# Context projection of the first pair first, eight early maxima of the second unit, one transpose for a unit's maxima

## The reference

```python
x = _layernorm(builder_state, g1, beta1)
base_n = _layernorm(base_state, g1, beta1)
q, k, v = (heads(q_in, Wq, bq), heads(kv_in, Wk, bk), heads(kv_in, Wv, bv))
scores = jnp.einsum('bhqd,bhkd->bhqk', q, k) * (1.0 / np.sqrt(HD))
attn = jax.nn.softmax(scores, axis=-1)
out = jnp.einsum('bhqk,bhkd->bhqd', attn, v)
x = residual + (out @ W_o.T + b_o)
U = (_layernorm(x, g2, beta2) @ W_in.T + b_in) @ Bmat
s = jax.nn.silu(s @ A.T) + u_t          # a scan over the rows
return x + states @ Cmat + mod
```

## Time and profile before

| what | value |
|---|---|
| median of three runs | 2315.91 us (2312.77 to 2317.89) |
| the profiled execution | 2315.49 us, span of its instructions 2313.7 us |
| TensorE busy | 2254.5 us, 97% of the span |
| VectorE busy | 1733.4 us, 75% |
| GpSimd busy | 1583.7 us, 68% |
| ScalarE busy | 1110.4 us, 48% |
| mean granted TensorE clock | 0.989 |

### The profile page before, as it was taken

The page is one execution under the profiler, slowest core; times in us unless marked ns, Lnnn a source line. Parts: engine busy times, 40 slices in busy tenths (PEclk is TensorE's granted clock), DMA queues, the critical chain, the costliest instruction groups (busy, mean ns, idle before and its releaser), DMA issues.

```text
span 2313.7 us, 36253 instructions
## 1 busy us (share of the span) xinstructions
PE 2254.5 (97%) x14262; PEld 1306.4 (56%) x14262; DVE 1733.4 (75%) x2167; ACT 1110.4 (48%) x1422; POOL 1583.7 (68%) x1039
## 2 busy tenths in 40 slices
PE   8999989999999999999999999999999999999987
PEld 8998854554555544555555455555555555445764
DVE  5765446888888778888888788888888888755865
ACT  3654424445445445444454544544544545453454
POOL 1200026888888888888888888888888888887312
PEclk8999999999999999999999999999999999999998
DMA  6660225677777777777777777677677776787723
GB/s 241 211 193 10 83 64 118 147 160 159 157 160 155 165 167 171 174 158 161 157 159 169 174 174 173 156 166 158 151 158 162 161 160 155 185 186 172 240 100 145
DMA packets 159703, 365.02 MB, mean 158 GB/s; under 512 B 23535, under 2 KB 63087, under 8 KB 158894
## 3 DMA queue, kind: packets, MB, share of 16 engines
q0 software_dynamic: 59904, 218.13, 46.2%
q1 hardware_dynamic: 99630, 144.59, 19.3%
HBM read 95.41 MB, written 49.02 MB: 62 GB/s over the span
## 4 chain that ended last, share of the span: by engine, by line
PE 81%; DMA 5%; POOL 4%; issue 4%; DVE 4%; ACT 1%; POOLq 0%; SPq 0%; DVEq 0%; ACTq 0%
PE ps L1303 28%; PE ps L1176 10%; PE ps L1278 7%; PE ps L1280 7%; PE ps L1282 7%; DMA acca<-pt 5%; PE ps L1140 4%; PE ps L1270 4%; PE ps L1158 3%; PE ps L1148 3%; POOL accp L533 3%; PE ps L1368 2%; PE ps L1121 1%; DVE mx_part L922 1%; PE ps L1425 1%
## 5 line engine op out<-in xcount | busy, mean ns | idle before, releaser
L715 ACT ACTIVATE pt<-ps 128x1024 f32<-128x1024 f32 x800 | 779.3, 1021 | 908.5 <-PE ps L1282 878.2
L922 DVE TENSOR_REDUCE mx_part<-ps 128x2 f32<-128x1024 f32 x768 | 938.0, 1221 | 338.5 <-PE ps L1176 338.4
L533 POOL TENSOR_TENSOR accp<-accp,pt 128x1024 f32<-128x1024 f32 x416 | 1040.5, 2501 | 220.7 <-ACT pt L715 219.0
L1303 PE MATMUL ps<-pt,v 128*64 128x512 f32 x3328 | 805.6, 605 | 0.0
L995 DVE TENSOR_TENSOR ps<-ps,shb 128x1024 f32<-128x1024 f32 x403 | 493.1, 1224 | 52.1 <-PE ps L1282 52.1
L1303 PEld LDWEIGHTS ps<-pt,v 128*64 128x64 f32 x3328 | 201.8, 136 | 344.0 <-issue 335.3
L1176 PE MATMUL ps<-kk,qh 64*128 64x512 f32 x1536 | 349.0, 450 | 10.0 <-DVE mx_part L922 10.0
L1176 PEld LDWEIGHTS ps<-kk,qh 64*128 64x128 f32 x1536 | 143.3, 183 | 355.2 <-DVE mx_part L922 268.6
L1278 PE MATMUL ps<-qh,kk 64*128 64x512 f32 x1664 | 328.8, 391 | 6.9 <-ACT pt L715 6.9
L1280 PE MATMUL ps<-qh,kk 64*128 64x512 f32 x1664 | 328.5, 390 | 0.0
L1282 PE MATMUL ps<-ql,kk 64*128 64x512 f32 x1664 | 328.2, 389 | 0.0
(11 more groups left out here) (154 smaller groups left out, 1898.3 us busy)
## 6 DMA issues: line engine op xcount, KB each, us to landing
acca<-pt POOLq DMA_DIRECT2D x224, 512.0 KB, 4.9
accb<-pt POOLq DMA_DIRECT2D x160, 512.0 KB, 4.8
q_scratch<-kk SPq DMA_DIRECT2D x32, 512.0 KB, 4.4
acca<-accp POOLq DMA_DIRECT2D x32, 512.0 KB, 4.6
o_scratch<-ost SPq DMA_DIRECT2D x32, 512.0 KB, 3.0
og<-o_scratch SPq DMA_DIRECT2D x32, 512.0 KB, 5.9
shb<-m_scratch SPq DMA_DIRECT2D x31, 512.0 KB, 4.1
xs<-x SPq DMA_DIRECT2D x16, 512.0 KB, 6.4
```

Of the source, the lines that this page charges most:

```text
L533: nc.gpsimd.tensor_tensor(acc[:, :], acc[:, :], pt[n % PT_SLOTS][:, :], ALU.add).then_inc(added_p, 1)
L715: nc.scalar.activation(pt[n % PT_SLOTS][:, :], src, ACT.Exp, scale=SCALE).then_inc(exped, 1)
L922: nc.vector.tensor_reduce(mx_part[:, m % QT, :, m // QT], src, AX_X, ALU.max).then_inc(max_taken, 1)
L1303: ins = mm(ps[HD * h:HD * (h + 1), 6, :], v[:, t, f:f + HD], pt[n % PT_SLOTS][:, h * QB:(h + 1) * QB], start=(t == 0), stop=(t == NT - 1))
```

## The change

- The chunks of K are projected in the order of the pairs, 2, 3, 0, 1. ScalarE's wait for the stored q in group 0 moves ahead of its first V copy.
- Eight maxima of unit 1 join those of unit 0 in the projection (`ctx_maxima`, 34 in all, `M_EARLY`): two in group 2, three in groups 3 to 11, five in the last. In a group the first stands behind the second K chunk, the second behind the second V product, the third behind the fourth K chunk. VectorE takes the first ahead of its four `low_k`, and the second and third behind them. All early maxima use banks 5 and 6. The eight have q in a tile of their own, `qx`, loaded behind `qh` of unit 0. `mx_part` gets a second buffer.
- In the last group the K chunks come first, with maxima between them, then V for the first half, the turn of unit 0's maxima, and V for the second half. ScalarE does `shift(0)` before both copies of V.
- Every unit, unit 0 too, has two maxima in each step: 18 of unit 1 and eight of unit 2 in unit 0. In its first step both tiles' scores stand ahead of the shift matmuls. The turn is at step 9 in every unit.
- `mx_row` is [128, 2 x 4], and a single transpose gives eight rows of 128 (bank 7, for unit 0 bank 0). ScalarE negates these into `shift_row`; SyncE stores them to DRAM, waits, and loads the two rows of 512 into `sh` (`send_shift`), and loads `shb` as before (`spread_shift`).

```diff
 M_LEAD = 4
-M_FIRST = NM + 2 * M_LEAD
+M_EARLY = NM + 2 * M_LEAD
 
 
 def maxima_of(u, j):
 
-    if u == 0:
-        first, last = M_FIRST * j // NJ, M_FIRST * (j + 1) // NJ
-    else:
-        first = M_FIRST + 2 * (NJ * (u - 1) + j)
-        last = first + 2
-    return [(i // NM + 1, i % NM) for i in range(first, min(last, NM * (UNITS - 1)))]
-
-
-def turn_step(u):
-
-    return NJ - M_LEAD if u else NM * NJ // M_FIRST + 1
+    first = M_EARLY + 2 * (NJ * u + j)
+    return [(i // NM, i % NM) for i in range(first, min(first + 2, NM * UNITS))]
+
+
+TURN_STEP = NJ - M_LEAD
...
+def ctx_maxima(g):
+
+    if g < 2:
+        return []
+    if g == C_G - 1:
+        return [(0, m) for m in range(21, NM)]
+    third = [(1, g - 3)] if 3 <= g < C_G - 2 else [(0, 20)] if g == C_G - 2 else []
+    return [(0, 2 * (g - 2)), (0, 2 * (g - 2) + 1)] + third
+
+
+EARLY = [p for g in range(C_G) for p in ctx_maxima(g)]
+
+
+def nth_max(w, m):
+
+    return EARLY.index((w, m)) if (w, m) in EARLY else NM * w + m
...
+def max_bank(w, m):
+
+    return 5 if (w, m) in EARLY else 4
+
+
+def turn_bank(w):
+
+    return 7 if w else 0
...
-        mxp = at("mxp", [P, QT, HD + 1], RR + 11776)
-        mx_part = at("mx_part", [P, QT, 2, 7], RR + 12040)
+        mx_row = at("mx_row", [P, 2, QT], RR + 11776)
+        mx_part = [at("mx_part0", [P, QT, 2, 7], RR + 12032), at("mx_part1", [P, QT, 2, 7], RR + 11784)]
+        shift_row = at("shift_row", [2 * QT, P], RR + 11840, F32R)
+        qx = at("qx", [P, QB], RR + 12096, F32R)
         oraw = at("oraw", [P, QB], RR + 12096)
-        lnb = at("lnb", [P, 64], RR + 12096)
+        lnb = at("lnb", [P, 64], RR + 11968)
...
             def store_k(g):
                 for p in (0, 1):
-                    sp.wait_ge(k_ready, FC * g + (p + 1))
+                    sp.wait_ge(k_ready, FC * g + PAIR_ORDER.index(p) + 1)
                     keys = slice(g * GW, (g + 1) * GW)
                     sp.dma_start(k_scratch[p][:, :, keys], kk[:, p, :, keys].bitcast(F32)).then_inc(k_stored, 16)
 
+            def send_shift(w):
+                sp.wait_ge(shift_ready, w + 1)
+                wait(sp, sh_loaded, 16 * (w - 1))
+                wait(sp, shb_loaded, 16 * (w - 2))
+                sp.dma_start(m_scratch[w % 2].rearrange("h (q k) -> (h q) k", k=P), shift_row[:, :].bitcast(F32)).then_inc(sh_stored, 16)
+                sp.wait_ge(sh_stored, 16 * (w + 1))
+                sp.dma_start(sh[w % 2][0:HD + 1:HD, :].bitcast(F32), m_scratch[w % 2]).then_inc(sh_loaded, 16)
+
             def spread_shift(w):
-                sp.wait_ge(shift_ready, w + 1)
-                sp.dma_start(m_scratch[w % 2], sh[w % 2][0:HD + 1:HD, :].bitcast(F32)).then_inc(sh_stored, 16)
-                sp.wait_ge(sh_stored, 16 * w)
                 wait(sp, shifted, tiles_added(w - 1))
...
+                    b, p = unit(1)
+                    sp.dma_start(qx[:, :].bitcast(F32), q_scratch[b, 0, p]).then_inc(qx_loaded, 16)
...
-            sp.wait_ge(proj_done, projected(NG - 1))
+            sp.wait_ge(proj_done, projected(NG - 1) - 2)
             load_ql(0)
             for w in (1, 2):
                 load_qh(w)
             store_k(C_G - 1)
+            sp.wait_ge(ones_set, 3)
+            send_shift(0)
...
+                    send_shift(u + 1)
                     spread_shift(u + 1)
...
             def take_v(g, t):
-                act.wait_ge(proj_done, projected(X_G + g - 1) + (1, 4)[t])
+                act.wait_ge(proj_done, projected(X_G + g - 1) + ((1, 4)[t] if g < C_G - 1 else (5, 6)[t]))
                 nc.scalar.activation(v[:, GT * g + t], ps[:, 7, :], ACT.Copy).then_inc(v_ready, 1)
 
-            def high_k(g, c):
-                act.wait_ge(proj_done, projected(X_G + g - 1) + (2, 3, 5, 6)[c])
-                nc.scalar.activation(kk[:, c, 0, g * GW:(g + 1) * GW], ps[:, 2 + c % 3, 0:GW], ACT.Identity,
+            def high_k(g, i):
+                c = PAIR_ORDER[i]
+                act.wait_ge(proj_done, projected(X_G + g - 1) + ((2, 3, 5, 6)[i] if g < C_G - 1 else i + 1))
+                nc.scalar.activation(kk[:, c, 0, g * GW:(g + 1) * GW], ps[:, 2 + i % 3, 0:GW], ACT.Identity,
                                      bias=bqkv[:, 1, c:c + 1]).then_inc(k_hi, 1)
+
+            def shift(w):
+                act.wait_ge(max_turned, w + 1)
+                wait(act, sh_stored, 16 * w)
+                nc.scalar.activation(shift_row[:, :], ps[0:2 * QT, turn_bank(w), 0:P], ACT.Copy, scale=-1.0)\
+                    .then_inc(shift_ready, 1)
 
             act.wait_ge(cols_loaded, 16)
             act.wait_ge(w_loaded[0], 16)
                     if g == 0:
                         act.wait_ge(bias_ready, 2)
                         act.wait_ge(wkv_lo, 2 * FC)
-                    take_v(g, 0)
-                    high_k(g, 0)
-                    if g == 0:
                         for half in (0, 1):
                             act.wait_ge(q_stored[half], 32 * (X_G // 2))
-                    high_k(g, 1)
-                    take_v(g, 1)
-                    high_k(g, 2)
-                    high_k(g, 3)
-
-
-            def shift(w):
-                act.wait_ge(max_turned, w + 1)
-                if w == 0:
-                    act.wait_ge(ones_set, 3)
-                nc.scalar.activation(sh[w % 2][0:HD + 1, :], ps[0:HD + 1, 7, :], ACT.Copy, scale=-1.0)\
-                    .then_inc(shift_ready, 1)
+                    if g < C_G - 1:
+                        take_v(g, 0)
+                        high_k(g, 0)
+                        high_k(g, 1)
+                        take_v(g, 1)
+                        high_k(g, 2)
+                        high_k(g, 3)
+            for i in range(FC):
+                high_k(C_G - 1, i)
+            shift(0)
+            for t in range(GT):
+                take_v(C_G - 1, t)
...
-            def low_k(g):
-                for c in range(FC):
-                    dve.wait_ge(k_hi, FC * g + (c + 1))
-                    nc.vector.scalar_tensor_tensor(out=kk[:, c, 1, g * GW:(g + 1) * GW], in0=ps[:, 2 + c % 3, 0:GW],
-                                                   scalar=bqkv[:, 1, c:c + 1],
-                                                   in1=kk[:, c, 0, g * GW:(g + 1) * GW].bitcast(F32),
-                                                   op0=ALU.add, op1=ALU.subtract).then_inc(k_ready, 1)
-
-            def take_max(w, m, i):
+            def low_k(g, i):
+                c = PAIR_ORDER[i]
+                dve.wait_ge(k_hi, FC * g + (i + 1))
+                nc.vector.scalar_tensor_tensor(out=kk[:, c, 1, g * GW:(g + 1) * GW], in0=ps[:, 2 + i % 3, 0:GW],
+                                               scalar=bqkv[:, 1, c:c + 1],
+                                               in1=kk[:, c, 0, g * GW:(g + 1) * GW].bitcast(F32),
+                                               op0=ALU.add, op1=ALU.subtract).then_inc(k_ready, 1)
+
+            def take_max(w, m):
                 if m == 0:
-                    wait(dve, max_ready, w)
-                dve.wait_ge(max_done, NM * w + (i + 1))
-                src = ps[:, 5:7, :] if w == 0 else ps[:, 4:6, :]
+                    wait(dve, max_ready, w - 1)
+                dve.wait_ge(max_done, nth_max(w, m) + 1)
+                b = max_bank(w, m)
...
             def row_max(w):
-                dve.wait_ge(max_taken, NM * (w + 1))
+                dve.wait_ge(max_taken, NM * (w + 1) if w else M_EARLY)
                 wait(dve, max_turned, w)
-                nc.vector.tensor_reduce(mxp[:, :, 0:HD + 1:HD], mx_part[:, :, :, :], AX_X, ALU.max).then_inc(max_ready, 1)
+                nc.vector.tensor_reduce(mx_row[:, :, :].rearrange("p h q -> p q h"), mx_part[w % 2][:, :, :, :], AX_X, ALU.max)\
+                    .then_inc(max_ready, 1)
...
-                    if g >= 2:
-                        take_max(0, 2 * (g - 2), 2 * (g - 2))
-                    low_k(g)
-                    if g >= 2:
-                        take_max(0, 2 * (g - 2) + 1, 2 * (g - 2) + 1)
-            for m in range(2 * (C_G - 2), NM):
-                take_max(0, m, m)
+                    early = ctx_maxima(g)
+                    if g < C_G - 1:
+                        for w, m in early[:1]:
+                            take_max(w, m)
+                        for i in range(FC):
+                            low_k(g, i)
+                        for w, m in early[1:]:
+                            take_max(w, m)
+            for i in range(FC):
+                take_max(*ctx_maxima(C_G - 1)[i])
+                low_k(C_G - 1, i)
+            take_max(*ctx_maxima(C_G - 1)[FC])
             row_max(0)
...
-            def maxima(w, m, i):
-
-
-                wait(pe, max_taken, NM * w + i)
-                if i == 0:
+            def maxima(w, m):
+
+                wait(pe, max_taken, nth_max(w, m))
+                if m == 0 and w == 1:
+                    pe.wait_ge(qx_loaded, 16)
+                elif m == 0 or (w, m) == (1, 2 * M_LEAD):
```

(97 more changed lines are left out.)

30 lines of the change are left out of this document (14 added, 16 removed).

## The result

The changed kernel takes 2320.43 us, the median of 20 runs (2316.32 to 2325.8), against 2315.78 us for the kernel before in as many runs on the same chip: ratio 1.0024 (1.0016 to 1.0032). It is a quarter of a per cent slower. The forecast was 0.17% faster, so the sign is wrong, by 8.4 us.

The account below looks back on a forecast made before the run. TensorE was taken to bound the projection and units 1 to 31, with waits only in the tail and unit 0. From 2315.5 us, -12.4 + 24.3 + 0.3 - 11.4 - 5.7 + 1.4 = -3.5 gave 2312 us, range 2303 to 2324.

Parts of the forecast that it names:

- A: Unit 0, steps 1 to 12: two maxima per step in place of mostly three, 52.8 us against 65.2, -12.4 us.
- B: Context groups 3 to 11: a third maximum costs 0.42 us plus a 2.28 us wait for VectorE, +24.3 us.
- E: End of group 11: one clock fall of 3.4 us, +1.4 us; the other groups keep the full clock.
- Rival 1: Context groups: the clock falls in every group's stall, eight falls more, +13.6 us, 2325.7 us; chance 0.15.
- C: Turns in units 1 to 30: one transpose in place of four saves 0.38 us each, -11.4 us.
- Rival 2: The turn: a lone transpose hides in the switch, -20.4 us in place of -11.4, put at 2305 us; chance 0.18.
- D: Tail, last group's start to step 1 of unit 0: 22.7 us in place of 28.4, -5.7 us.
- Rival 4: Shift row through DRAM: late in every unit behind POOL's accumulations, 0.5 us in 31 units, 2327 us; chance 0.05.
- Rival 3: Context groups: no stall, because VectorE gets to the second maximum sooner, 2290 us; chance 0.09.

Follow-up runs that it names:

- the four useless matmuls: The changed kernel with four matmuls whose result nothing uses ahead of the third early maximum in groups 3 to 11: 2316.59 us, ratio 1.0004 to the kernel before.
- the turn alone: The kernel before with only one transpose in place of four and the shift row through DRAM, in every unit: 2304.03 us, ratio 0.9949.
- the orders without the stall: Changed kernel, VectorE taking the second maximum before the third chunk's low part: 2293.7 us; also with TensorE's second maximum between third and fourth K products: 2292.33 us.

## Why the prediction was wrong

**A, unit 0: right.** -12.3 against -12.4; no step waits.

**B, the third maximum: mechanism right, term too small.** The chain, its place and its releaser are as read from the earlier trace rows; idle 2.31 against 2.28. But the third maximum costs 0.61 in place of 0.42 and the stall 2.39 in place of 2.28. The 0.42 is a distance of two starts, and the work behind a maximum is slower too, which that row can't show. Nine times (3.00 - 2.70) are 2.7 us. The trace of the kernel before had the right price of a maximum; these are the transposes with which its groups 1 to 3 begin:

```profile
156.73 1.04 PE L1121 MATMUL ps<-ident,xs 128*128 128x128 f32 x8
168.84 1.04 PE L1121 MATMUL ps<-ident,xs 128*128 128x128 f32 x8
...
182.13 1.09 PE L1121 MATMUL ps<-ident,xs 128*128 128x128 f32 x8
```

Group 1, without a maximum, takes 12.11 us, group 2, with two, 13.29: 0.6 for each. The prediction read the pair's distance instead.

**E, the clock: this step failed.** "The other groups keep it" rested on one wait that left the clock alone. That wait was 2.21 us long (up to 2020.04), hardly shorter than the stalls of 2.31, so it was one case of the right length that happened to bring no fall. Rival 1 had the mechanism. Of its ground, the thin work behind the stall, the four useless matmuls show that it is not enough by itself. The clock fell in the stalls of groups 3, 5, 7, 9 and 11, one fall having been forecast, that of group 11. The others cost nearly all of the 6.5 us in 153.7, 1.6 each, as I had priced them (1.7). I asked whether such a wait makes a fall; the right question was how many of nine do. The answer here is every second one: rival 1, with all of them at 2325.7, was too high by 5.3 us, the forecast too low by 8.4. It set its point of decision at five more falls, 2320.5 us; four, together with the 2.7 of B, brought the time to 2320.4, just short of it. The one fall that E did forecast was mis-sized too: it held 6.8 us, not 3.4, and cost an estimated 2.2 us behind group 11, half of TensorE's 4.5 busy us in it, where E had 1.4.

**C, the turn: right.** The order of time in unit 1, last scores, transpose, next maximum:

```profile
452.77 0.39 PE L1337 MATMUL ps<-ql,kk 64*128 64x512 f32 x2
453.09 0.27 PE L1242 MATMUL ps<-ident,mx_row 128*8 128x128 f32 x1
453.29 0.50 PE L1221 MATMUL ps<-kk,qh 64*128 64x512 f32 x2
```

453.29 - 452.77 = 0.52 against 0.90: -0.38, as worked out. Rival 2 (nearly nothing is left) is out: a turn keeps 0.30. There are 0.7 us beyond the 11.4. TensorE waited 7.9 us for ScalarE's exponentials in units 1 to 31 before and 6.1 now, 1.8 less; where the other 1.1 of this went isn't traced.

**D, the tail: right.** 24.9 us against 22.7 + 1.4. The wait of 1.41 in front of 336.88 is the one forecast; the K product behind it ran at the lower level and took 2.93 for 1.7. Without the 2.2 us of the longer fall (E) the tail is the 22.7 us forecast; the missing gain of 0.8 belongs to E. The shift row left ScalarE and went over DRAM like this (SyncE's issues):

```profile
351.11 0.50 SPq L387 DMA_DIRECT2D m_scratch<-shift_row  x1
353.93 0.59 SPq L389 DMA_DIRECT2D sh<-m_scratch  x1
```

The store and its signal took 2.8 us. The matmuls that use the row started at 357.00, right behind the scores, 0.23 after their predecessor (356.77), so the load, issued at 353.93, was there within 3.1. Rival 4 (a late row) is out in the changed kernel; without the scores ahead of it, it costs 1.64 us once, as the turn alone showed.

**The sum again.** -12.3 (A) + 27.0 + 6.5 (B and four falls) - 12.1 (C) - 3.5 (D, E) - 2.0 (elsewhere) = +3.6 us, against -3.5. Elsewhere, 1.1 us less lie ahead of the context groups and 1.7 less behind unit 31. The change does nothing in either place, and over all eleven traces the first spreads over 1.6 us and the second over 3.5, so this is chance. Group 0 gives 0.6 back: TensorE waits 0.32 there for the V copy (150.53), the 0.3 forecast, and the group takes 12.69 us (143.57 to 156.26) against 12.11 (144.62 to 156.73). The other 1.3 of the 8.4 us come from the median, which lies 1.2 above the profiled execution, and from rounding. Rival 3 (no stall) was wrong for this kernel, but its 2290 us is near what the orders without the stall took, 2293.7 and 2292.3.

## What to carry to other kernels

When a change puts a request for a shared buffer into the program of one engine, find the same item in the program of the engine that frees the buffer. Here TensorE's second maximum had moved ahead of two K products, VectorE's had stayed behind all four low parts, and that order alone took 28 us. A bottleneck engine's short, regular stall is to be priced twice, with its idle time and with what the clock may cost behind it, and one wait in the trace that did no harm is no evidence for nine. A small piece of work set between long products costs more than the distance from its start to the next: compare whole groups that have it with groups that don't.

## What the runs showed of the hardware

- Stalls of TensorE of 2.31 us in otherwise dense work brought the granted clock from 1.00 to 0.50, from the level of 2.4 GHz to that of 1.2, in every second group of the changed kernel and not in the ones between; seven extra matmuls, once, took away the first of these falls, and eleven moved them from odd to even groups. Stalls of 1.38 us didn't in eight groups (behind the ninth, with a second wait of 1.41 us, a fall came), stalls of 3.57 did in nine of nine. Each count is from one execution. The Trainium skill ("TensorE: Matmul & The Clock Gate", A second HAM failure mode: psum-queue depth-cycling) tells of a bf16 kernel that cycles through PSUM banks: TensorE is idle for short spells between groups of matmuls, often enough to make the clock oscillate between its two levels. The changed kernel's trace agrees, with 0.91 over the groups that begin with a fall and 0.99 to 1.00 over the others.
- A fall held 3.4 us and cost 1.6 inside the changed kernel's groups; where the stall was 3.57 us it held 6.8 and cost 2.9. Behind group 11 of the changed kernel, where a second wait of 1.41 us followed the stall, it held 6.8 as well. Why some falls are longer isn't shown.
- A transpose of eight columns has a weight load of 83 ns, one of 65 columns 138. The rule of the section LDWEIGHTS of the same page of the Trainium skill, columns over 1.2 in nanoseconds, gives 47 ns between the two as an estimate; the traces have 55. So the slope about agrees, but the loads themselves are 76 and 84 ns longer than the rule's 7 and 54. None of it reached TensorE's path: the turn got shorter by three spacings and nothing else.
